# Node scores of a graph network's front: VectorE on rows of 400 nodes in place of transposes and products

## What is computed

```python
score = X @ p / jnp.linalg.norm(p)
top_vals, top_idx = jax.lax.top_k(score, c)          # c = 128
X_tilde = X[top_idx] * jnp.tanh(top_vals)[:, None]
W = _gru_step(X_tilde, W0, w_ih, w_hh, b_ih, b_hh)
XW = X @ W
```

## Time and profile before

| | |
|---|---|
| time, median of 3 runs | 3558.3 us (3554.54 to 3558.34) |
| profiled execution, first to last instruction (its span) | 3856.9 us |
| the front in it, until the node pass starts | 498.4 us |
| PE / DVE / ACT / POOL busy over the span | 79% / 71% / 60% / 65% |

### The profile page before, as it was taken

How to read it: one execution, slowest core, us unless ns; L and a number is a source line. 1 busy time by engine, 2 the same in 40 slices (tenths; PEclk the granted TensorE clock), 3 DMA queues, 4 the chain that set the end, 5 groups by cost and what they waited for, 6 DMA issues and landing times. The chain is left out here.

```text
span 3856.9 us, 54369 instructions
## 1 busy us (share of the span) xinstructions
PE 3033.4 (79%) x11490; PEld 2023.8 (52%) x11490; DVE 2725.5 (71%) x6900; ACT 2299.0 (60%) x5259; POOL 2523.9 (65%) x2721
## 2 busy tenths in 40 slices
PE   3124149999999998899979999979999996777676
PEld 2012035555555555777759999955555553343333
DVE  3005749999999998777769989969999994222222
ACT  2003039999999999777623333439999994232332
POOL 5750069999999998777534444436666763666665
PEclk7557569999999999899989999989999997777777
DMA  5012025555555554444323343322322321222221
GB/s 190 1 36 90 1 76 171 171 168 169 171 164 175 164 176 141 113 123 119 109 86 112 114 112 110 109 81 72 88 83 84 86 82 44 72 73 72 72 68 46
DMA packets 262118, 404.65 MB, mean 105 GB/s; under 512 B 61938, under 2 KB 104135, under 8 KB 262033
## 3 DMA queue, kind: packets, MB, share of 16 engines
q1 hardware_dynamic: 204920, 304.18, 24.6%
q0 software_dynamic: 44032, 73.90, 8.4%
q10 hardware_dynamic: 13081, 25.69, 2.0%
HBM read 213.15 MB, written 194.37 MB: 106 GB/s over the span
## 5 line engine op out<-in xcount | busy, mean ns | idle before, releaser
L256 POOL TENSOR_TENSOR dn_rstd<-dn_var,w_minus_half 128x4 f32<-128x4 f32 x294 | 292.6, 1002 | 16.7 <-DVE dn_var L241 16.5
L1603 POOL DMA_INDIRECT m_src<-table_x,e_src_first x196 | 191.1, 975 | 127.5 <-issue 52.1
L1603 POOL DMA_INDIRECT p_src<-table_x,e_src x196 | 213.1, 1087 | 93.0 <-issue 53.6
L2491 POOL DMA_INDIRECT out_rows<-m_x,e_out_first x196 | 197.6, 1008 | 94.0 <-issue 65.8
L648 POOL DMA_INDIRECT scratch_node_row<-o_own,e_out x196 | 192.0, 979 | 90.7 <-issue 62.4
L1643 POOL DMA_INDIRECT g_own<-in_x,e_dst x196 | 223.9, 1142 | 36.9 <-issue 36.9
L2576 DVE TENSOR_TENSOR m_y<-m_bout,m_own 128x512 f32<-128x512 f32 x49 | 33.9, 692 | 294.3 <-DMA a_typ<-in_type_row 166.3
L1603 POOL DMA_INDIRECT a_src<-table_x,e_src x196 | 200.9, 1025 | 47.6 <-issue 37.5
L1634 POOL DMA_INDIRECT g_src<-scratch_wide,e_src x196 | 192.0, 980 | 58.8 <-issue 46.0
L1409 PE MATMUL n_banks<-w_gru_both,d_xT 128*128 128x256 f32 x784 | 223.6, 430 | 8.6 <-ACT d_xT L1446 8.6
L1409 PEld LDWEIGHTS n_banks<-w_gru_both,d_xT 128*128 128x128 f32 x784 | 192.9, 327 | 71.3 <-ACT d_xT L1446 68.6
(11 more groups left out here) (486 smaller groups left out, 9952.8 us busy)
## 6 DMA issues: line engine op xcount, KB each, us to landing
table_x<-d_x SPq DMA_DIRECT2D x294, 256.0 KB, 2.0
g_src<-in_x_wide SPq DMA_DIRECT2D x97, 262.0 KB
scratch_wide<-g_src SPq DMA_DIRECT2D x97, 262.0 KB
out_rows<-d_x SPq DMA_DIRECT2D x97, 256.0 KB
s_x<-in_x ACTq DMA_DIRECT2D x31, 768.0 KB
table_x<-d_xT SPq DMA_DIRECT2D x49, 256.0 KB
scratch_post<-d_x SPq DMA_DIRECT2D x49, 256.0 KB, 2.0
p_rc<-scratch_rcount SPq DMA_DIRECT2D x49, 256.0 KB
```

Of the source, the lines that this page charges most:

```text
L256: pool.tensor_tensor(self.rstd[s][:], self.var[s][:], minus_half[:], ALU.pow).then_inc(self.rooted[s], 1)
L1603: pool.indirect_dma_start(out=self.rows[s][:, t * P:(t + 1) * P], out_offset=None, in_=self.table, in_offset=bass.IndirectOffsetOnAxis(ap= ...
L2491: pool.indirect_dma_start(out=D["out"], out_offset=bass.IndirectOffsetOnAxis(ap=Ed.out_first[:, at:at + 1], axis=0), in_=x4[s][:, t * P:(t ...
```

## The change

The scores are made on DVE alone. x is taken as 125 partitions of 400 consecutive nodes each (125 is the largest divisor of 50000 up to 128), in 25 chunks of 16 nodes: 125 x 2048 elements, 8 KB contiguous to a partition, 1 MB to a transfer. A chunk is multiplied in place with p, which is loaded to all partitions, and summed over the features into 16 columns of `score`, now 128 x 400. The loads stay with ACT, six buffers deep; from the seventh on each waits until a buffer's chunk is summed. Transposes, copies, score products, the window and the move are gone. The number of a node is now 400 times the partition plus the place.

DVE's order is new: chunks lie between the parts of the row scan, the tables and the fold; the fold's 13 block copies have a chunk ahead of each. The fold's last two parts (`vector_last`, `vector_rows`) are moved behind the first level of lists and the first merged list. PE has its small products in the same order, with nothing between. ACT issues nine loads, makes the root of the tables, and issues the rest.

```diff
+        self.LANES = max(n for n in range(1, P + 1) if nodes % n == 0)
+        self.PER_LANE = nodes // self.LANES
+        self.CHUNK = max(n for n in range(1, 17) if self.PER_LANE % n == 0)
+        self.CHUNKS = self.PER_LANE // self.CHUNK
...
+    BUFS = 6
+    x = [mem.sb(f"s_x{b}", [P, CHUNK * P]) for b in range(BUFS)]
+    p = mem.sb("s_p", [P, P])
...
     def load(act, j):
+        if j >= BUFS:
+            act.wait_ge(summed, j - BUFS + 1)
+        src = bass.AP(tensor=A["x"].tensor, offset=j * CHUNK * P, ap=[[PER_LANE * P, LANES], [1, CHUNK * P]])
+        act.dma_start(x[j % BUFS][0:LANES, :], src).then_inc(loaded[j % BUFS], 16)
...
+    def vector(dve, j):
+        rows = x[j % BUFS][0:LANES, :].rearrange("p (r f) -> p r f", f=P)
+        dve.wait_ge(loaded[j % BUFS], 16 * (j // BUFS + 1))
+        dve.tensor_tensor(rows, rows, each(p[0:LANES, :], CHUNK), ALU.mult).then_inc(weighed, 1)
+        dve.wait_ge(weighed, j + 1)
+        dve.tensor_reduce(score[0:LANES, j * CHUNK:(j + 1) * CHUNK], rows, AX, ALU.add).then_inc(summed, 1)
...
         best(score, v1, i1)
         numbered(n1i, i1, n1, basef[:, 0:1])
+        fold["vector_last"](dve)
         for n, r in enumerate(ROWS):
             dve.wait_ge(lists_loaded, 16 * (n + 1))
             best(merged[n], vm[n], im[n])
             if n == 0:
                 numbered(fmi[n], im[n], fm[n], basef[0:r, n + 1:n + 2])
+                fold["vector_rows"](dve)
...
         @block.vector
         def _(dve):
-            marks["vector"](dve)
             rows["vector_begin"](dve)
             tables["vector_begin"](dve)
-            marks["vector_window"](dve)
+            marks["vector_begin"](dve)
+            marks["vector"](dve, 0)
             rows["vector"](dve)
+            marks["vector"](dve, 1)
+            rows["vector_carry"](dve)
+            marks["vector"](dve, 2)
+            rows["vector_enter"](dve)
+            marks["vector"](dve, 3)
             tables["vector"](dve)
             rows["vector_last"](dve)
             tables["vector_first"](dve)
+            marks["vector"](dve, 4)
+            marks["vector"](dve, 5)
             fold["vector"](dve)
+            for b in range(13):
+                if b < plan.CHUNKS - 6:
+                    marks["vector"](dve, 6 + b)
+                fold["vector_block"](dve, b)
+            for k in range(3):
+                fold["vector_sum"](dve, k)
+                for j in (19 + 2 * k, 20 + 2 * k):
+                    if j < plan.CHUNKS:
+                        marks["vector"](dve, j)
+                fold["vector_own"](dve, k)
+            fold["vector_std"](dve)
...
             top["vector"](dve)
...
         @block.scalar
         def _(act):
-            marks["begin"](act)
-            for j in range(Q):
-                if j == 5:
-                    tables["scalar_root"](act)
-                marks["copy"](act, j)
-            marks["move"](act)
+            first = min(marks["ahead"] + 3, plan.CHUNKS)
+            for j in range(first):
+                marks["load"](act, j)
+            tables["scalar_root"](act)
+            for j in range(first, plan.CHUNKS):
+                marks["load"](act, j)
```

More of the change, by code:

```diff
@@ L473, in gpsimd @@
                            pattern=[[depth, HEADS], [0, depth]], channel_multiplier=-1).then_inc(made, 1)
-    def vector(dve):
[L476 to L506, removed]
@@ new lines, in fold_weights, with then, centre, constant @@
+    steps = [0]
+    def then(dve, ins):
+        ins.then_inc(step, 1)
+        steps[0] += 1
+        dve.wait_ge(step, steps[0])
+    def centre(dve, out, src):
+        mean = sums[0:src.shape[0], :]
+        then(dve, dve.tensor_reduce(mean, src, AX, ALU.add))
+        then(dve, dve.tensor_scalar(mean, mean, -1.0 / P, None, ALU.mult))
+        then(dve, dve.tensor_scalar(out, src, mean, None, ALU.add))
+    def constant(dve, c, r):
+        then(dve, dve.tensor_copy(crow[:, c * P:(c + 1) * P], r))
@@ new lines, in split @@
+    def split(dve, out, x, member):
+        n, m = x.shape
+        high, middle, low, sum_ = (part3[k][0:n, 0:m] for k in range(4))
+        then(dve, dve.tensor_copy(high, x))
+        then(dve, dve.tensor_tensor(x, x, high, ALU.subtract))
+        then(dve, dve.tensor_copy(middle, x))
+        then(dve, dve.tensor_tensor(x, x, middle, ALU.subtract))
+        then(dve, dve.tensor_copy(low, x))
+        then(dve, dve.tensor_scalar(sum_, high, member[0], None, ALU.mult))
+        then(dve, dve.scalar_tensor_tensor(sum_, middle, member[1], sum_, ALU.mult, ALU.add))
+        then(dve, dve.scalar_tensor_tensor(sum_, low, member[2], sum_, ALU.mult, ALU.add))
+        then(dve, dve.tensor_copy(out, sum_.rearrange("p (c f) -> p c f", f=P).unsqueeze(2).to_broadcast([n, m // P, TPG, P])
+                                  if m > P else sum_))
@@ L518, in vector @@
[L518 to L525, removed]
@@ L528, in vector @@
[L528 to L547, removed]
@@ new lines, in vector @@
+        centre(dve, W.g1c[:], W.g1c[:])
+        then(dve, dve.tensor_scalar(W.w1_ffn[:], raw["w1"][:], cols[:, G1:G1 + 1], None, ALU.mult))
+        then(dve, dve.tensor_tensor(row[:], rows[0:1, R_BE1, :], rows[0:1, R_B2_FFN, :], ALU.add))
+        centre(dve, row[:], row[:])
+        constant(dve, C_FFN, row[:])
+        centre(dve, row[:], rows[0:1, R_B2_MSG, :])
+        constant(dve, C_MSG, row[:])
+        then(dve, dve.tensor_copy(bias_wide[:].rearrange("p (h d) -> p h d", h=HEADS), over(bias8[:], P // HEADS)))
@@ new lines, in vector, with vector_block, vector_sum @@
+        split(dve, W.head_bias[:], bias_wide[:], [W.split[:, k + 1:k + 2] for k in range(3)])
+    def vector_block(dve, b):
+        dve.wait_ge(block_made, b + 1)
+        to = X_BLOCK if b == 0 else stat_block((b - 1) % STATS, (b - 1) // STATS)
+        dve.tensor_copy(W.post[:, to, :], bank[b % 2][:, 0:P]).then_inc(block_copied, 1)
+    def vector_sum(dve, k):
+        if k == 0:
+            dve.wait_ge(block_copied, 13)
+        mx, mn, mean = (W.post[:, stat_block(n, k), :] for n in (MX, MN, MEAN))
+        then(dve, dve.tensor_tensor(csum[:], mx, mn, ALU.add))
+        dve.tensor_tensor(csum[:], csum[:], mean, ALU.add).then_inc(csum_made, 1)
+        then(dve, dve.tensor_scalar(mn, mn, -1.0, None, ALU.mult))
@@ new lines, in vector_own @@
+    def vector_own(dve, k):
+        dve.wait_ge(own_made, k + 1)
+        then(dve, dve.tensor_copy(W.own[:, k, :], bank[2][:, 0:P]))
+        then(dve, dve.tensor_copy(row[:], bank[3][0:1, 0:P]))
+        if k == 0:
+            centre(dve, rows[0:1, R_B_LIN, :], rows[0:1, R_B_LIN, :])
+            then(dve, dve.tensor_tensor(rows[0:1, R_B_LIN, :], rows[0:1, R_B_LIN, :], bank[3][0:1, P:2 * P], ALU.add))
+            then(dve, dve.tensor_tensor(row[:], row[:], rows[0:1, R_B_LIN, :], ALU.add))
+        constant(dve, C_PNA + k, row[:])
@@ L705, in vector, with vector_carry, then @@
         dve.tensor_tensor_scan(whole[:], keep[:], zeros[:], 1.0, ALU.mult, ALU.add).then_inc(ends, 1)
+    def vector_carry(dve):
+        def then(ins):
+            ins.then_inc(step, 1)
+            steps[0] += 1
+            dve.wait_ge(step, steps[0])
         dve.wait_ge(lined, 1)
@@ L711, in vector, with vector_enter, then @@
         dve.tensor_tensor_scan(carry[:, 1, 1:], line[:, 2, :], line[:, 1, :], 0.0, ALU.mult, ALU.add).then_inc(carried, 1)
+    def vector_enter(dve):
+        def then(ins):
+            ins.then_inc(step, 1)
+            steps[0] += 1
+            dve.wait_ge(step, steps[0])
         dve.wait_ge(entered, 1)
@@ L929, in begin @@
-    def begin(act):
-        for j in range(min(BUFS, Q)):
-            load(act, j)
-    pieces = []
-    for q in range(4):
-        count = max(0, min(Q, plan.NF - q * Q))
-        if count:
-            pieces.append((32 * q, count, slice(0, GROUP)))
-        if q * Q <= plan.NF < (q + 1) * Q and plan.NF < plan.NG:
-            last = slice(0, N - plan.NF * GROUP)
-            pieces = [p for p in pieces if p[0] != 32 * q] + [(32 * q, count + 1, last)]
-            if count:
-                pieces.append((32 * q, count, slice(last.stop, GROUP)))
@@ L944, in move @@
-    def move(act):
-        act.wait_ge(cleared, 1)
-        act.wait_ge(scored, Q)
-        for first, count, cols in pieces:
-            act.copy(score[first:first + count, cols], bank_score[first:first + count, cols]).then_inc(moved, 1)
+    def vector(dve, j):
[4 more added lines that the diff above has]
+        dve.tensor_reduce(score[0:LANES, j * CHUNK:(j + 1) * CHUNK], rows, AX, ALU.add).then_inc(summed, 1)
@@ L951, in done, with top_nodes @@
     def done(eng):
-        eng.wait_ge(moved, len(pieces))
-    return dict(sync=sync, vector=vector, vector_window=vector_window, turn=turn, product=product, copy=copy, begin=begin, move=move, done=done)
-def top_nodes(nc, A, D, W, plan, score, scored, weight, bank):
+        eng.wait_ge(summed, CHUNKS)
```

(22 more changed lines are left out.)

117 lines of the change are left out of this document (36 added, 81 removed).

## The result

The changed kernel takes 3666.22 us (median of 4 runs, 3664.60 to 3670.13) against 3556.42 us for the kernel before on the same chip: ratio 1.0314, interval 1.0299 to 1.0328, 110 us slower. The forecast was 3651, range 3596 to 3692.

A forecast was written before the change was run, and what follows sets the result against it. POOL's scatters end the old front at 289 us; x on five DMA engines brings scores at 219, plus 136 for top-k and 26.2 behind it, 382. So +93 on 3558.3 gives 3651 us, range 3596 to 3692.

The forecast's parts named there:

- late hand-overs: Front, 46 to 280 us: slow passing of work between engines, taken to belong to the profiled execution only; front 289, not 498.4.
- The mark for the scores: Front of kernel before with prompt hand-overs: scores ready near 115 us; the new way costs nothing down to about 128.
- the cover: Front of kernel before: VectorE's names were to be ready 13 us before POOL, which ends the front, needs them.
- Chunks: VectorE's score work: 25 products of 2.28 us and sums of 2.26, with gaps 4.6 us a chunk, 115 in all.
- The fold pieces as cost-free: Between chunks on VectorE: 41 us of old work, hidden by x's 214 us load, so no cost.
- The load of x: Front: 125 partitions run on five of sixteen DMA engines, 127.5 GB/s, 201 us; last chunk lands near 214 us.
- The first maximum: Start of VectorE's top-k chain: near 219 us, after the last chunk's landing near 214 and its product and sum.
- The top-k chain: VectorE, first maximum to the 128 names: 133.8 us less 5.4 for fewer columns plus 7.6 for moved fold, 136 us.
- All sixteen engines: Rival on x's load: all engines carry the chunks, VectorE's own 170 us end the scores; +43, 3601 us; chance 0.13.
- Slower stream: Rival on x's load: 21 GB/s an engine, or fold weights at 130 us; 3674 to 3694 us; chance 0.10.
- T0: In the slower-stream rival: when the scores are ready for the top-k chain, 240 to 262 us against 219 forecast.
- Late hand-overs in every execution: Rival on the front: timed runs also end it at 498 us, the change at 382; -116, 3442 us; chance 0.11, whole.

The follow-up runs named there:

- the two runs with fills: Kernel before plus 10 or 40 idle memsets on VectorE between scores and first maximum: 3559.70 us (ratio 1.0019) and 3597.26 us (ratio 1.0127).

## Why the prediction was right

**What bounds.** Right, and decisive. The reading that the first profile's late hand-overs are not in the runs gave a front of 289 us; 290.4 was measured, and 90 instead of 77 for the message stage. Read by the span alone, the change is a gain: 3665.0 against 3856.9.

**The mark for the scores.** The first maximum of before was set at 115 and came at 123.1, and the names at 257.2 instead of 249. POOL's end, 261.9, came as 263.2. So the cover was 6.6 us where the sum had 13, and the two runs with fills bear that out. It made no difference, since the change overran it by a hundred.

**Chunks.** Right to 1%: 2.29 and 2.29 us, against 2.28 and 2.26. The fold pieces as cost-free: nearly; without the products, 57 us less work gave 3 of time.

**The load of x.** Right: 25 x 5 small packets, a DMA share of 0.3, 131 GB/s (127.5 forecast, 114 to 136 allowed). The split by 112 and 13 partitions shows that the engines are the cause.

**The first maximum.** 236.3 against 219: the term that was mis-sized, by 17 us. It has three parts. The pause in the stream is 7.8 us (the run with nine buffers); the step had called six buffers enough, with the fold weights at 90 us, and they came at 104.9. Between the end of the last sum (231.7) and the first maximum stand 4.6 us, where the sum had nothing: 2.6 of small pieces of the fold and 2.0 of preparations of the top-k chain, which in the kernel before lay under the wait for the scores. The rest, 17.3 - 7.8 - 4.6 = 4.9, no run shows by itself; this is an estimate. With nine buffers the last chunk is there at 219.5 us. 25.6 MB at 131 GB/s are 195 of them, so the start and the other loads took 24 us where the step had 2 + 11 = 13. Two rows of the DMA view of after are near that: q1's 6.7% of 240 us is 16 us an engine, q0's 1.4%, the scatters, which the step left out, is 3. The stream itself was 5 us better than forecast, which by luck hid half of it.

**The top-k chain.** 372.7 - 236.3 = 136.4; 136 forecast. Behind the names 26.6 us, forecast 26.2.

**POOL.** Covered, as said, but its own end was 309.9 and not 277: it started 6.6 us later, at 55.6, and the scatters were longer. With a cover of 63 us it costs nothing; with the split load the cover is 16.

**Sum.** The front moved from 290.4 to 399.3, 109 us; 110 were timed and 93 forecast. The missing 17 are those of the first maximum.

**The rivals.** *All sixteen engines* is what the split load makes; it was given 3601 and took 3612, the fold weights being late there too (12.2 us of wait). *Slower stream* was out by its rate, though its second half (late fold weights) held in part; from T0 240 its own sum gives 3672, not 3674, and the range ends 2 us short of its 3694. *Late hand-overs in every execution*: the second profile of the same kernel, at 3553.27 us, is without them, and so are the later ones.

## What to carry to other kernels

Before costing anything, compare the span of the profile with the times of the runs: where they differ by more than the runs scatter, find the stretches that are late and make the sum without them. Work that is moved to a free engine can lose by the shape of its load: count the partitions of each transfer, and the small packets in its queue. Here 125 split into 112 and 13 took some 52 of 110 us off. And an end set by one engine's queue, as POOL's 176 scatters here, leaves only its start worth moving: removing all of the scores gave 7 us, starting the scatters 3.9 us sooner 4.6 (1.4 to 7.8).

## What the runs showed of the hardware

**Engines by partitions.** Transfers over 125 partitions left 5 small packets each and ran at 131 GB/s; over 112 and 13 they left 29 and ran at some 235, until the buffers were full. This is the rule that the prediction cites from the Trainium skill; trace and rule agree, in both kernels.

**Small loads beside long packets.** The fold weights, on another queue, were ready at 104.9 us beside 8 KB packets on five engines, and at 71.5 beside the same packets on sixteen. 36.6 us of VectorE's time went into the wait, while its buffers filled. The queues of after up to 105 us:

```profile
q10 hardware_dynamic: 1454, 11.46, 27.6%
q1 hardware_dynamic: 4435, 3.77, 12.9%
```

That is some 280 long packets on each of five engines and 277 small ones on each of sixteen, nearly one for one, as the prediction's step had it; it had set 250 small ones, and nothing for their own time, which is 13.5 us an engine by this row. It is no rule: beside sixteen engines, up to 72 us, 4501 small packets stand beside 12.29 MB of x, 281 an engine beside some 94 long ones.

**Scatters beside two-operand products.** POOL's scatters in after, and the products of DVE in the same stretch:

```profile
116.00 0.98 POOL L661 DMA_INDIRECT scratch_node_row<-o_own,e_out  x1 [0.30 <-issue]
117.28 2.23 POOL L661 DMA_INDIRECT scratch_node_row<-o_own,e_out  x1 [0.30 <-issue]
119.81 0.98 POOL L661 DMA_INDIRECT scratch_node_row<-o_own,e_out  x1 [0.30 <-issue]
121.09 0.98 POOL L661 DMA_INDIRECT scratch_node_row<-o_own,e_out  x1 [0.30 <-issue]
122.37 1.89 POOL L661 DMA_INDIRECT scratch_node_row<-o_own,e_out  x1 [0.30 <-issue]
```

```profile
116.14 0.18 DVE L506 COPY w_head_bias<-f_part 24x128 bf16<-24x128 bf16 x1
116.36 2.29 DVE L915 TENSOR_TENSOR s_x<-s_x,s_p 125x2048 f32<-125x2048 f32 x1
118.69 2.29 DVE L917 TENSOR_REDUCE score<-s_x 125x16 f32<-125x2048 f32 x1
121.09 2.33 DVE L915 TENSOR_TENSOR s_x<-s_x,s_p 125x2048 f32<-125x2048 f32 x1
```

A scatter that starts within a product ends 0.84 to 0.86 us after that product's end (119.51 after 118.65, 124.26 after 123.42), in 21 cases of 21; one that starts with it, within 0.01 us (121.09), or beside a sum, which reads one array, takes its 0.98. Without products none is over 1.15, and the 176 take 22.6 us less from the first to the last. The Trainium skill, page "SBUF — State Buffer", section "SBUF: two separate sides", describes a pair of ports that a VectorE operation with two inputs in SBUF and a GpSimd operation that reads SBUF can only hold in turn, the first to start for its whole length. The trace agrees for the scatters and not for the products: at 116.36 one starts 0.36 us into a scatter, right behind the copy before it, and takes its 2.29. In this kernel it cost nothing, behind 63 us of cover. In one that POOL bounds, such as the kernel before, I expect that the same products would cost time; no run put them there.
